# Expert weights' rows read from one SBUF partition each

## The reference, cut to what matters

```python
x_lat = x @ fc1_w.T                                      # 1024 x 128
h = relu2(jnp.einsum('tl,eil->eti', x_lat, w1))          # 32 experts, 128 inner values
h = h * cw.T[:, :, None]                                 # one weight per token and expert, mostly 0
y_lat = jnp.einsum('eti,eli->tl', h, w2)                 # sum over experts
routed = y_lat @ fc2_w.T
shared = relu2(x @ shared_up_w.T) @ shared_down_w.T
return (shared + routed).reshape(orig_shape)
```

## Time and profile before

| | us |
|---|---|
| median of 3 runs (lowest, highest) | 550.75 (550.51, 550.77) |
| the profiled execution | 551.04 |
| its span (first to last recorded instruction) | 549.2 |
| TensorE busy in it | 533.3 |
| VectorE, ScalarE, GpSimd busy | 384.7, 355.8, 324.3 |
| mean granted clock of TensorE | 1.00 of full speed |

### The profile page before, as it was taken

The page is one execution under the profiler, slowest core; times in us unless marked ns, Lnnn a source line. Parts: engine busy times, 40 slices in busy tenths (PEclk is TensorE's granted clock), DMA queues, the critical chain, the costliest instruction groups (busy, mean ns, idle before and its releaser), DMA issues.

```text
span 549.2 us, 9661 instructions
## 1 busy us (share of the span) xinstructions
PE 533.3 (97%) x3234; PEld 454.9 (83%) x3234; DVE 384.7 (70%) x821; ACT 355.8 (65%) x749; POOL 324.3 (59%) x325
## 2 busy tenths in 40 slices
PE   8999999999999999999999999999999999889997
PEld 6778867778788988988898999999999778668786
DVE  4867997799765676565646586756764868768873
ACT  5562146868687768676757565746766766777881
POOL 2679355998387787655635324435887547762230
PEclk9999999999999999999999999999999999999999
DMA  8910254510266877876676666534545735356751
GB/s 271 375 71 24 65 179 135 193 40 20 91 209 201 226 229 231 265 222 213 214 235 217 207 206 202 182 102 142 190 156 162 239 104 199 108 163 172 224 176 38
DMA packets 66544, 94.73 MB, mean 172 GB/s; under 512 B 6336, under 2 KB 38976, under 8 KB 66496
## 3 DMA queue, kind: packets, MB, share of 16 engines
q1 hardware_dynamic: 66496, 94.12, 54.6%
HBM read 66.71 MB, written 27.39 MB: 171 GB/s over the span
## 4 chain that ended last, share of the span: by engine, by line
PE 68%; DVE 9%; POOL 8%; ACT 5%; issue 5%; DMA 3%; SPq 1%; DVEq 0%; ACTq 0%; POOLq 0%
PE ps L1646 20%; PE ps L1647 20%; PE ps L1648 19%; PE ps L1779 4%; DMA cw_row<-cw_scratch 2%; PE ps L1875 1%; DMA xr<-in_x 1%; DVE e_r L1559 1%; POOL inner L657 1%; DVE st L1137 1%; PE ps L1891 1%; DMA k_hl<-k_scratch 1%; POOL inner L656 1%; POOL fly L651 1%; POOL fly L652 1%
## 5 line engine op out<-in xcount | busy, mean ns | idle before, releaser
L676 POOL TENSOR_TENSOR probs<-probs,rsum 128x512 f32<-128x512 f32 x64 | 66.5, 1043 | 55.1 <-DVE rsum L1333 55.0
L1328 DVE TENSOR_REDUCE nmax<-ps 128x2 f32<-128x512 f32 x64 | 44.0, 688 | 31.3 <-PE ps L1648 30.9
L1012 ACT ACTIVATE probs<-ps,nmax 128x256 f32<-128x256 f32 x128 | 59.9, 481 | 1.7 <-DVE nmax L1328 1.6
L1097 ACT ACTIVATE e_hi<-e_r 128x512 fp32r<-128x512 f32 x64 | 40.2, 629 | 28.3 <-DVE e_r L1559 27.6
L593 POOL TENSOR_TENSOR kv_w_lo<-blk_raw,kv_w_hi 128x1024 fp32r<-128x1024 f32 x16 | 38.8, 2426 | 23.9 <-ACT kv_w_hi L845 23.9
L1319 DVE TENSOR_TENSOR pT_lo<-ps,pT_hi 128x512 fp32r<-128x512 f32 x64 | 43.8, 686 | 12.0 <-ACT pT_hi L1018 11.5
L799 POOL TENSOR_TENSOR e_lo<-e_sq,e_hi 128x512 fp32r<-128x512 f32 x19 | 24.6, 1295 | 44.5 <-ACT e_sq L1103 39.6
L1559 DVE SCALAR_TENSOR_TENSOR e_r<-ps,cw_row 128x512 f32<-128x512 f32 x64 | 43.3, 684 | 10.1 <-PE ps L1648 5.5
L1324 DVE TENSOR_TENSOR oT_lo<-ps,oT_hi 128x512 fp32r<-128x512 f32 x32 | 22.1, 692 | 39.7 <-ACT oT_hi L1022 39.7
L1018 ACT ACTIVATE pT_hi<-ps 128x512 fp32r<-128x512 f32 x64 | 38.3, 601 | 17.1 <-PE ps L1779 17.0
L599 POOL TENSOR_TENSOR k_hl<-k_hl 128x512 fp32r<-128x512 f32 x20 | 25.9, 1297 | 39.5 <-ACT k_hl L937 37.3
(11 more groups left out here) (314 smaller groups left out, 1864.6 us busy)
## 6 DMA issues: line engine op xcount, KB each, us to landing
cw_row<-cw_scratch SPq DMA_DIRECT2D x64, 256.0 KB, 3.6
v_hl<-v_scratch SPq DMA_DIRECT2D x24, 512.0 KB, 3.7
blk_raw<-in_w_blocks SPq DMA_DIRECT2D x22, 512.0 KB, 4.4
k_scratch<-kv_out SPq DMA_DIRECT2D x32, 256.0 KB, 3.5
v_scratch<-kv_out SPq DMA_DIRECT2D x32, 256.0 KB, 3.2
v_scratch<-kv_hi SPq DMA_DIRECT2D x24, 256.0 KB, 2.6
k_hl<-k_scratch SPq DMA_DIRECT2D x12, 512.0 KB, 3.4
k_hl<-k_scratch SPq DMA_DIRECT2D x20, 256.0 KB, 4.8
```

Source lines behind the costliest of these rows:

```text
L676: nc.gpsimd.tensor_tensor(probs[:, b, :, :], probs[:, b, :, :], rsum[:, b, :].unsqueeze(2).to_broadcast([P, 2, S]), ALU.mult).then_inc(pro ...
L1012: last = nc.scalar.activation(probs[:, b, t, :], ps[:, S_BANK[b], t * S:(t + 1) * S], ACT.Exp, bias=nmax[:, b, t:t + 1], accum_out=esum[:, ...
L1097: nc.scalar.activation(e_hi[i % 4][:, :], e_r[i % 2][:, :], ACT.Square).then_inc(e_hi_done, 1)
L1328: V.tensor_reduce(nmax[:, b, :], ps[:, S_BANK[b], :].rearrange("p (t k) -> p t k", t=2), AX.X, ALU.max, negate=True).then_inc(max_done, 1)
```

## The change

The second half of what SyncE does is left, with another source; its first half is gone. Task "C" turns each tile's 128 tokens x 32 experts by itself, in four transposes side by side in one PSUM bank, so that partition `e` holds all 512 tokens of expert `e`. ScalarE copies these 32 x 512 values into partitions `g * 32` to `g * 32 + 31` of a single tile `cwT` (64 x 512). `load_row(i)` reads row `i` of this tile, one SBUF partition, 128 times over into the 128 partitions of `cw_row[i % 4]`. `cw_scratch`, its eight stores and the semaphore `cw_stored` are gone; where SyncE waited for the stores, it waits for `cwT_done`, ahead of row 0 and of row 32.

```diff
-        cwT = [sb(f"cwT{g}", [P, P]) for g in range(NG)]
+        cwT = sb("cwT", [NG * E, GT])
...
-            scratch = cw_scratch.rearrange("e (g j p) -> e g j p", g=NG, j=GN)
-
-            def store_weights(g):
-
-                sp.wait_ge(cwT_done, g + 1)
-                for j in range(GN):
-                    sp.dma_start(scratch[:, g, j, :], cwT[g][j * E:(j + 1) * E, :]).then_inc(cw_stored, 16)
-
             def load_row(i):
 
                 g, e = i // E, i % E
                 if i >= 4:
                     sp.wait_ge(root_done, i - 3)
-                sp.dma_start(cw_row[i % 4][:, :], cw_scratch[e:e + 1, g * GT:(g + 1) * GT].broadcast_to([P, GT])).then_inc(ld_cw[i % 4], 16)
+                sp.dma_start(cw_row[i % 4][:, :], cwT[i:i + 1, :].unsqueeze(1).to_broadcast([1, P, GT])).then_inc(ld_cw[i % 4], 16)
...
                 if TASK_IN_STEP.get("e" + str(u)) == ("C", 0):
-                    store_weights(0)
-                    sp.wait_ge(cw_stored, 16 * GN)
+                    sp.wait_ge(cwT_done, 1)
                     for i in range(4):
                         load_row(i)
...
             for i in range(4, NI):
-                if i == E - 1:
-                    store_weights(1)
-                elif i == E:
-                    sp.wait_ge(cw_stored, 16 * GN * NG)
+                if i == E:
+                    sp.wait_ge(cwT_done, NG)
                 load_row(i)
...
             def weights_back(g, bank):
                 act.wait_ge(cwT_filled, g + 1)
-                nc.scalar.activation(cwT[g][:, :], ps[:, bank, 0:P], ACT.Copy).then_inc(cwT_done, 1)
+                nc.scalar.activation(cwT[g * E:(g + 1) * E, :], ps[0:E, bank, :], ACT.Copy).then_inc(cwT_done, 1)
...
                     pe.wait_ge(cw_ready, g + 1)
-                    nc.tensor.transpose(ps[:, bank, 0:P], cw[:, :, :].rearrange("p n e -> p (n e)"), ident).then_inc(cwT_filled, 1)
+                    for j in range(GN):
+                        last = nc.tensor.transpose(ps[0:E, bank, j * P:(j + 1) * P], cw[:, j, :], ident)
+                    last.then_inc(cwT_filled, 1)
```

More of the change, by code:

```diff
@@ L6, in flamingo_two_layer_kernel @@
 def flamingo_two_layer_kernel(nc, x, ids, ctx_t, g_xattn, g_ffn, w_gate_t, w_up_t, w_down_t,
-                              w_blocks, w_tail, gate_w_t, gate_bias, fc1_t, fc2_t, ident_in, had_in, cw_scratch, k_scratch, v_scratch, out, batches):
+                              w_blocks, w_tail, gate_w_t, gate_bias, fc1_t, fc2_t, ident_in, had_in, k_scratch, v_scratch, out, batches):
     F32, F32R, BF16, I32 = mybir.dt.float32, mybir.dt.float32r, mybir.dt.bfloat16, mybir.dt.int32
@@ L250, in flamingo_two_layer_kernel @@
         ld_cw = [sem(f"ld_cw{i}") for i in range(4)]
-        cw_stored, out_stored = sem("cw_stored"), sem("out_stored")
+        out_stored = sem("out_stored")
         dve_step, pool_step = sem("dve_step"), sem("pool_step")
@@ L2200 @@
     args = [nc.dram_tensor(k, v.shape, mybir.dt.from_np(v.dtype), kind="ExternalInput").ap() for k, v in arrays.items()]
-    experts = a["L1_ffn_gate_w"].shape[0]
-    scratch = nc.dram_tensor("cw_scratch", (experts, T), mybir.dt.float32, kind="Internal").ap()
     k_scratch = nc.dram_tensor("k_scratch", (2, heads, P, 2, T // 2), mybir.dt.float32, kind="Internal").ap()
@@ L2205 @@
     out = nc.dram_tensor("out", (T, D), mybir.dt.float32, kind="ExternalOutput").ap()
-    flamingo_two_layer_kernel(nc, *args, scratch, k_scratch, v_scratch, out, B)
+    flamingo_two_layer_kernel(nc, *args, k_scratch, v_scratch, out, B)
     r = run_bass_kernel_spmd(nc, [arrays], core_ids=[0])
```

## The result

The changed kernel takes 992.33 us (median of 4 runs, 988.26 to 992.75), the kernel before 550.63 beside it: a ratio of 1.801, 95% interval 1.798 to 1.804. The forecast was 1075 us, with a range of 975 to 1210.

A forecast was written before the change was run, and what follows sets the result against it. The kernel before was taken as bound by TensorE's matmuls, the changed one by rows: 415.7 first issue + 1.5 landing + 642 for 64 rows + 3.8 blocks and results + 10 tail = 1073, plus 1.8 = 1075 us; range 975 to 1210.

The forecast's parts named there:

- part 3: Source of the 64 row loads: one SBUF partition read 128 times, taken as deciding, 10.0 us a row.
- The mechanism: In the row loads: one SBUF partition gives one 2 KB piece at a time, 78.4 ns each.
- The price of a row: Row loads of the expert units: 10.03 us for each of 64 rows, 642 us in the sum.
- the forecast's 0.76: Chance given to row loads costing 8.6 to 12 us each, 985 to 1201 us in all.
- (b): Rival for the row loads: a partition gives several but fewer than six pieces at once; 550 to 985 us; chance 0.08.
- The start: Ahead of the expert units: first row issued at 415.7 us, 415.0 plus 0.66 for the turn.
- Part 2: The turn: four transposes span 0.60 us against 0.27, copy 0.27 to about 0.60; 0 to 0.7 us in all.
- Part 1: Eight stores leave SyncE's queue: 1.9 us saved at row 31's wait, vanishing once SyncE isn't what rows wait for.
- The tail: After the last row lands at 1063: 2.7 us on its values, then 7.3 to the end, 10 us together.
- (a): Rival for the row loads: rows keep up, row 31 no longer behind four stores; 549 us, 1.9 faster; chance 0.08.
- (c): Rival for the row loads: dearer than one piece after another, 13.8 us a row, 1316 us; chance 0.06.
- (d): Rival for the turn: rows keep up, stores were hidden, four transposes cost 0.7 us; 551.5 us; chance 0.02.

The follow-up runs named there:

- the turn without the source: Against the kernel before: the change's turn, rows still through memory outside the chip, one 64 KB store in place of four of 16; 549.76 us, ratio 0.9997.

## Why the prediction held, step by step

**The bound and the place** (part 3) were right: rows became what everything waits for, at some 27 GB/s from one place of SBUF. The late blocks came as written (the five weight blocks behind rows land after 21.2 us, 5.0 before). The other signs came in part: rows land after 27.4 us, not 30 to 40; L1548 waits 7.3 us on average, not 9; the gaps are even but for one in four; and the rate is 27 to 34 GB/s in slices with rows alone, for the reason below. From a rate well over 26 the prediction would have read that a partition serves several engines at once; the runs give another reason, rows of two outlets that overlap.

**The mechanism** was right in its effect and not in its wording. The prediction had one partition giving one piece at a time. The runs show a rate, shared by partitions 0 to 3 and by 0 and 32, while some 14 engines have a piece open. And its 78.4 ns are what an engine moved in the fullest 2 us, where transfers from outside the chip ran as well (a weight block is issued at 15.2), so that the reason it gave for preferring them to 108 ns doesn't hold. That 26.1 GB/s of one engine and 27.3 of one outlet lie so close was luck as far as the runs go: none shows why they should be alike. Nor were "three rows still on their way" behind the landed one: SyncE's held issue let some two. That cost nothing, since two are enough to keep one outlet busy.

**The price of a row** is the term that was mis-sized: 10.03 us forecast, 8.73 measured, which makes most of the 83 us between 1075 and 992. Of the 1.30 us, 0.4 is the outlet's rate, 27.3 GB/s and not 26.1; I had the trace's fullest 2 us, which is no limit of anything. The other 0.9 is the sentence "whether two of them could be read side by side nothing here shows, and I count no gain". Neighbouring rows are not read side by side, but every fourth row belongs to another outlet, and the overlap there saves 63 x 9.62 - 550.2 = 56 us over all rows, 3.7 for each of the 15 changes of group. The run on partition 0 (and 32), which has no such change, took 1051.5 us, close to 433 + 64 x 9.65 = 1050.6. The measured 992 lies only 7 us above the 985 at which the forecast's 0.76 began and rival (b) ended: a little more overlap would have made it (b)'s time. That it stayed on the forecast's side is in part luck, since the overlap was counted at nothing. The 3.8 us for blocks and results lie within the 550.2 and can't be told apart.

**The start** was right: first row issued at 415.9 (415.7 forecast), first unit at 428.0 (427.2). Part 2's sizes too: four transposes span 0.60 us, the copy takes 0.588. **Part 1's** saving was rightly called lost.

**The tail** was 12.8 us, not 10. The low part of row 62 stands behind L1548 of row 63 on VectorE's list, and that came when row 63 landed, at 978.2. So TensorE stood still for 7.0 us, and two experts' products with shared ones between them came after the last row, where the sum had the last expert's alone. Those up to 983.5 also ran at the lower level of its clock. From 600 to 700 us, where the engine was busy for 38 of 100 us, it was granted 0.62 on average; at 980 it had 0.50, which is 1.2 GHz, and by 984 1.00, which is 2.4 GHz, TensorE having been busy without a gap since 979.5. A product's matmul took 0.63 us at the one level and 0.40 at the other. Stretches, then instructions in order of time:

```profile
980.00:982.00 2.00, 2.00 (x8) 1.71 (x8) 0.69 (x1) 0.04 (x1) 0.00 (x0) 0.50 0.00 0
984.00:986.00 2.00, 2.00 (x17) 1.91 (x16) 0.76 (x2) 0.66 (x2) 0.00 (x0) 1.00 0.00 0
```

```profile
978.20 0.69 DVE L1548 SCALAR_TENSOR_TENSOR e_r<-ps,cw_row 128x512 f32<-128x512 f32 x1 [2.80 <-DMA cw_row<-cwT]
978.80 0.68 DVE L1558 TENSOR_TENSOR e_lo<-ps,e_hi 128x512 fp32r<-128x512 f32 x1
979.54 0.79 PE L1635 MATMUL ps<-e_hi,ex_lo 128*128 128x512 f32 x1 [7.00 <-DVE e_lo L1558]
...
980.56 0.63 PE L1637 MATMUL ps<-e_hi,ex_hi 128*128 128x512 f32 x1
...
984.08 0.40 PE L1637 MATMUL ps<-e_hi,ex_hi 128*128 128x512 f32 x1
...
987.60 1.40 SPq L551 DMA_DIRECT2D out<-xr  x3
```

Elsewhere TensorE waited for rows at either level, so the clock should have cost little there; no run shows it by itself.

**The rivals.** (a), faster by 1.9 us, fell with the rows. Its own sum was off as well: the two versions that kept 1.1 and 0.5 us of the wait, with no late start, are level with the kernel before. The 1.9 us were read from one execution; 12 runs against 23 don't show them. (b) had one partition giving several pieces at once. That isn't seen, one partition stays at 9.7 us a row; what comes to the same is several outlets side by side, for the 56 us above in the changed kernel and for 3.9 to 5.2 us a row where rows are spread, 2.8 with copies. (c) didn't come. (d) is answered by the turn without the source: its ratio is 0.9997.

## What to carry to other kernels

Transfers that read one SBUF partition, or its neighbours in a group of four, were paced here by one outlet of 27 GB/s, though some 14 DMA engines had pieces open and up to four rows were asked for: before moving a broadcast's source on the chip, divide its bytes by that rate and compare with the pace of its consumer (here 9.6 against 1.74 us). Broadcasts read from memory outside the chip have no such limit here and land in 3.6 us. If the source must be SBUF, lay rows that are on their way together in different groups of four partitions, and not 32 apart, and split them over two issuing queues, but expect two to four outlets' worth and not the sum. Look at how long each issue takes: where it is held, everything behind it on that engine's list is held too.

## What the runs showed that was not expected

Outlets that are free are not used in full: four rows on four outlets ran at 56 to 60 GB/s, eight at 66 to 69, with two lists 74 to 80 and about 100. And the issue of a row from SBUF occupies SyncE's list for 0.55 us at the least, that of a row from outside the chip for 0.32; while earlier rows are read slowly it grows to 9.13 us at the median, and a weight block behind them is held as long.
